# Rows of the first expert visit gathered on TensorE instead of through memory, in a two-layer graph and mixture-of-experts network

## What is computed

```python
scores = softmax(xt @ wg + bg)                       # 1024 x 8
routing_weights, selected = top_2_with_jitter(scores)
for e in range(8):
    h = gelu(xt @ w1[e]) * (xt @ w3[e])              # 512 -> 1024
    out = out + comb[:, e:e+1] * (h @ w2[e])         # 1024 -> 512
```

## Time and profile before

| | us |
|---|---|
| median of 3 runs | 1915.27 |
| lowest and highest | 1909.77, 1923.55 |
| the profiled execution | 1906.49 |
| its span in the profile | 1904.7 |

### The profile page before, as it was taken

One profiled execution on the slowest core, in us unless ns is written; L12 is line 12 of the kernel. 1 busy time (PEld: TensorE's weight loads), 2 busy tenths in 40 slices (PEclk: granted clock), 3 DMA queues, 4 the chain that ended last, 5 costly groups with the idle time before them and its releaser, 6 DMA issues.

```text
span 1904.7 us, 19746 instructions
## 1 busy us (share of the span) xinstructions
PE 1707.0 (90%) x7679; PEld 1322.5 (69%) x7679; DVE 1101.8 (58%) x1835; ACT 673.7 (35%) x879; POOL 1000.7 (53%) x546
## 2 busy tenths in 40 slices
PE   6998999999896699999998299999999859999996
PEld 5664567788764456788886178787777747887863
DVE  7597758999875476756327433423433266623275
ACT  3323534332421244243331255655555412221112
POOL 3224561466778667548860456667676480152402
PEclk9999989999999688899999599999999979999988
DMA  8362111455332211122351767787777341121001
GB/s 331 95 207 50 1 1 48 122 111 111 62 78 22 23 1 1 23 67 45 66 160 34 260 204 264 250 275 246 247 270 240 136 122 45 45 89 43 24 1 45
DMA packets 146780, 212.56 MB, mean 112 GB/s; under 512 B 43740, under 2 KB 60352, under 8 KB 145440
## 3 DMA queue, kind: packets, MB, share of 16 engines
q1 hardware_dynamic: 98736, 177.49, 28.6%
q0 software_dynamic: 42832, 18.84, 8.3%
q10 hardware_dynamic: 5120, 14.99, 2.3%
HBM read 187.21 MB, written 30.08 MB: 114 GB/s over the span
## 4 chain that ended last, share of the span: by engine, by line
PE 65%; DVE 14%; POOL 6%; DMA 5%; ACT 5%; issue 4%; SPq 0%; POOLq 0%; DVEq 0%
PE PS L634 17%; PE PS L636 17%; PE PS L635 17%; PE PS L799 5%; PE PS L813 3%; DMA table_c<-edge_add,edge_ix 2%; POOL table_w L2293 2%; POOL table_c L2293 2%; PE PS L790 2%; ACT kd L1308 2%; PE PS L782 2%; DMA table_w<-edge_add,edge_ix 1%; POOL W L2218 1%; DVE h_op L1946 1%; POOL slots_x L2327 1%
## 5 line engine op out<-in xcount | busy, mean ns | idle before, releaser
L2218 POOL TENSOR_TENSOR W<-raw,W 128x2048 fp32r<-128x2048 f32 x40 | 192.4, 4813 | 330.8 <-ACT W L1158 323.6
L2293 POOL DMA_INDIRECT table_w<-edge_add,edge_ix x128 | 208.6, 1630 | 69.8 <-DMA table_w<-edge_add,edge_ix 39.7
L2293 POOL DMA_INDIRECT table_c<-edge_add,edge_ix x128 | 204.6, 1598 | 60.8 <-issue 33.5
L634 PE MATMUL PS<-op_b,W 128*128 128x512 f32 x576 | 225.5, 392 | 3.6 <-DVE op_b L2025 2.6
L635 PE MATMUL PS<-op_b,W 128*128 128x512 f32 x576 | 224.4, 390 | 0.0
L636 PE MATMUL PS<-op_b,W 128*128 128x512 f32 x576 | 224.4, 390 | 0.0
L634 PE MATMUL PS<-W,op_a 128*128 128x512 f32 x480 | 188.2, 392 | 2.9 <-DVE op_a L1755 1.8
L635 PE MATMUL PS<-W,op_a 128*128 128x512 f32 x480 | 187.1, 390 | 0.0
L636 PE MATMUL PS<-W,op_a 128*128 128x512 f32 x480 | 187.0, 390 | 0.0
L2332 POOL TENSOR_TENSOR W<-raw,W 128x2048 fp32r<-128x2048 f32 x30 | 143.5, 4792 | 56.4 <-ACT W L1389 56.4
L1158 ACT ACTIVATE W<-raw 128x2048 fp32r<-128x2048 f32 x40 | 76.5, 1920 | 158.6 <-PE PS L636 103.3
(11 more groups left out here) (419 smaller groups left out, 3824.2 us busy)
## 6 DMA issues: line engine op xcount, KB each, us to landing
raw<-in_L_ffn_w_dram SPq DMA_DIRECT2D x46, 1024.0 KB, 5.7
raw_e<-in_L_ffn_w_dram SPq DMA_DIRECT2D x22, 1024.0 KB, 5.9
raw_v<-in_L_ffn_w_dram SPq DMA_DIRECT2D x22, 1024.0 KB, 5.2
raw<-in_L_mix_W_dram SPq DMA_DIRECT2D x16, 1024.0 KB, 6.7
raw<-table_c SPq DMA_DIRECT2D x10, 1024.0 KB, 5.2
key_row<-key_dram SPq DMA_DIRECT2D x32, 256.0 KB, 4.0
w_row<-in_edge_weight_dram SPq DMA_DIRECT2D x32, 256.0 KB, 4.8
table_w<-zero POOLq DMA_DIRECT2D x4, 1024.0 KB, 7.9
```

The lines of the kernel that those rows point to most:

```text
L634: pe.matmul(ps, lhs_hi, rhs_hi, start=start, stop=False)
L2218: pool.tensor_tensor(lo_at, raw[:, r % 2, :], hi_at.bitcast(F32), ALU.subtract).then_inc(lo_done, 1)
L2293: pool.indirect_dma_start(out=tb, out_offset=bass.IndirectOffsetOnAxis(ap=edge_ix[:, i, c:c + 1].bitcast(U32), axis=0), in_=edge_add[:, i, ...
```

## The change

Four things change.

1. `expert_of` is computed before `slot_ix`: the seven instructions L1879 to L1887 are written after L1902.
2. The rows of visit 0 no longer come through memory. POOL writes the numbers 0 to 255 into `iota_v`. DVE takes for each token the smaller of its two slots (`slot_min`) and compares: `pick[:, t, s]` is 1 where token t*128+p has slot s, else 0, in eight instructions. PE multiplies the tiles of G, taken as the stationary operand, with `pick` in plain float32: 4 column blocks of G x 8 token tiles = 32 matmuls of 128x256. They give the transposed rows of visit 0 in two banks, and ACT and DVE split them into `x_op` as before.
3. SP no longer loads `x_slot` for visit 0. Its wait for `scattered_x` and the load for visit 1 stand ahead of block 5 instead of block 4. ACT and DVE split the rows of visit 0 after blocks 0 and 1 instead of after 0, 1 and 2. ACT's wait for `scattered_x` ahead of block 3 stays.
4. The eight matmuls with `ones` in job `rank` use float32r operands: `chosen` has that type, and ACT copies `ones` to `ones_r` once.

```diff
@@ SP
-                if b == RING:
+                if b == RING + 1:
                     sp.wait_ge(scattered_x, 16 * 2 * NT)
-                    load_x_slots(0)
                     load_x_slots(1)
@@ PE
+            pe.wait_ge(ones_ready, 1)
             for t in range(NT):
-                mm = pe.matmul(bank(n)[:, (t + 1) * EXPERTS:(NT + 1) * EXPERTS].rearrange("p (t e) -> p t e", e=EXPERTS), ones[:, :],
+                mm = pe.matmul(bank(n)[:, (t + 1) * EXPERTS:(NT + 1) * EXPERTS].rearrange("p (t e) -> p t e", e=EXPERTS), ones_r[:, :],
                                chosen[:, t, :].unsqueeze(1).to_broadcast([P, NT - t, EXPERTS]), start=False, stop=(t == NT - 1))
...
-            x_transposes(0)
-            evacuated("xT0", visit_tiles(0))
+            for j in range(2):
+                n = JOB["xT0"] + j
+                open_job(n)
+                for k in (2 * j, 2 * j + 1):
+                    for t in range(NT):
+                        if k == 0:
+                            pe.wait_ge(pick_ready, t + 1)
+                        mm = pe.matmul(bank(n)[:, (k % 2) * 2 * P:(k % 2 + 1) * 2 * P], G[:, t, k * P:(k + 1) * P], pick[:, t, :],
+                                       start=(t == 0), stop=(t == NT - 1))
+                mm.then_inc(job_full, 1)
+            evacuated("xT0", 2)
@@ ACT
-            for b in range(RING - 1):
+            for b in range(2):
                 block_to_hi(b)
-            x_hi(0)
-            block_to_hi(RING - 1)
+            for j in range(2):
+                n = JOB["xT0"] + j
+                act.wait_ge(job_full, n + 1)
+                act.activation(x_op[:, 0, :, 0, 2 * j * P:2 * (j + 1) * P].rearrange("p i (k s) -> p k i s", k=2),
+                               bank(n).rearrange("p (k i s) -> p k i s", k=2, i=2), ACT.Copy).then_inc(job_act, 1)
+            for b in range(2, RING):
+                block_to_hi(b)
@@ DVE
+            dve.wait_ge(iota_ready, 1)
+            link(dve.tensor_tensor(slot_min[:, :], slot_f[:, 0, :], slot_f[:, 1, :], ALU.min))
+            for t in range(NT):
+                dve.tensor_scalar(pick[:, t, :], iota_v[:, :], slot_min[:, t:t + 1], None, ALU.is_equal).then_inc(pick_ready, 1)
```

50 lines of the change are left out of this document (33 added, 17 removed).

## The result

| | before | after |
|---|---|---|
| median of 12 runs, us | 1916.29 | 1903.68 |
| lowest and highest | 1904.39, 1928.45 | 1894.94, 1911.79 |
| span of the profiled execution | 1904.7 | 1899.7 |
| ratio after / before | | 0.9928, 95% interval 0.9902 to 0.9954 |

The kernel became faster by 13.8 us by the ratio (12.6 by the medians). The forecast was 1898.3 us in 1889 to 1908, with a gain of 17.0 us. The time is in the range, and it is within 1% of before, the likeliest of the three cases; about 3 us of the forecast's gain are missing. The times alone don't show that they are: the interval of the ratio is a gain of 8.8 to 18.8 us, which has the 17.0 in it. What is missing is read from the traces.

A forecast was written before the change was run, and what follows sets the result against it. PE was taken to set the pace, standing 36.3 us until visit 0's rows were loaded. 15.3 + 2.5 - 0.8 = 17.0 us off the median 1915.27 gave 1898.3 us, range 1889 to 1908 (1893 to 1903 from the gain alone).

The forecast's parts named there:

- What bounds the kernel: Expert stage: once visits run, PE sets their pace, so a later start of visit 0 ends the kernel equally later.
- Rival D: Later visits, bound by weights, give back visit 0's earlier start, so no effect; chance 0.02.
- Rank: Job rank on PE: float32r leaves one record for each product, 8 fewer at 0.21 us, 1.7 us less.
- Experts before slots: DVE in routing: `expert_of` ready 3.4 us earlier, `slot_ix` 1.5 us later.
- Picks and gather: Ahead of visit 0: first pick about 0.5 us after `slot_ix`, then every 0.29; PE's 64 gather records take 16.1 us.
- Rival B: PE's clock stays at 1.2 GHz in the gather, which takes 27.5 us; gain 4 to 6.3 us; chance 0.07.
- g0 of visit 0: Its first product on PE starts at 1074.4 instead of 1089.75, 15.3 us earlier.
- Up to g0 of visit 1: Visit 0's 15.3 us plus 2.5 us of its first products at full clock: 17.8 us, less 0 to 0.4.
- S: Time at which the scatter has landed, 1082.56 before; forecast from 1084.1 to 1086.7.
- Rival A: The scatter lands only at 1088 to 1094 and holds visit 0; gain 9 to 15 us; chance 0.13.
- What is late next: Visit 1's rows and blocks 3 to 5 wait for the scatter; 0.5 us off, with 0.3 for small things.
- Rival C: Slower: the later scatter, sharing engines with a fifth block, lands after 1101.6 and delays g0 of visit 1; chance 0.02.

The follow-up runs named there:

- e3: The changed kernel with the eight products of job rank in plain float32 again; ratio to before 0.9950.
- e4: The kernel before with only `expert_of` computed ahead of `slot_ix`; ratio to before 1.0019.
- e2: The changed kernel with the slots computed ahead of the experts again; ratio to before 0.9918.
- e1: The changed kernel with DVE's gating of visit 0's second half of hidden rows ahead of the low part of block 6; ratio to before 0.9921.
- c1: The changed kernel once more, unedited, for the spread; ratio to before 0.9929.
- f6: The changed kernel with ACT's gelu of g0 of visit 0 ahead of the high part of block 3; ratio to before 0.9880.
- f3: The changed kernel with DVE waiting for the scatter's end before the low part of block 2; ratio to before 0.9851.
- h4: h2 plus f3's wait of DVE for the scatter before the low part of block 2; ratio to before 0.9910.
- h2: The changed kernel with the orders of e1 and f6, and ACT making visit 1's rows ahead of block 6; ratio to before 0.9877.
- f4: The changed kernel with SP's wait for the scatter back ahead of block 4; ratio to before 0.9939.
- f1: e1 plus six thrown-away products on PE between job rank and the gather; ratio to before 0.9913.
- h1: h2 plus the six thrown-away products of f1; ratio to before 0.9912.

## Why the prediction was right, and where it was off

- **What bounds the kernel: right.** The visits kept their pace. The later waits are the same in both traces (1.01 and 0.69 us in turn), and what was gained at 80.8 is there at the end of the visits, 14.6 and 14.7 us. Rival D is out.
- **Rank, 1.7 us: right at the gather.** 1.85 us for 8 records; e3 gives the 1.7 back there. Further on it isn't shown.
- **Experts before slots: right in its times.** `expert_of` starts at 8.4 from chosen instead of 11.9, 3.4 us earlier, as forecast; `slot_ix` at 10.1 instead of 9.0, 1.1 us later (forecast 1.5). That the step is a loss by itself, and no gain with the rest of the change as it stands, the forecast didn't say; e4 and e2 show it.
- **Picks and gather: right.** The first pick 0.28 us after `slot_ix`, then 0.27 us each; 64 records in 16.23 us (forecast 16.1), the clock up after 4.4 us (forecast 4). Rival B is out.
- **g0 of visit 0: right.** 15.4 us earlier (forecast 15.3), and its products 0.23 us apart from the first on. Before, g0 to the first 0.69 us wait took 2.5 us over the clean 49.0; that is the forecast's 2.5 us of clock.
- **Up to g0 of visit 1: right.** 17.4 us earlier, against 17.8 less up to 0.4.
- **S: right.** Forecast were 1084.1 to 1086.7, which is 38.3 to 40.9 from chosen; it was 39.3 and 39.6. That is in part luck, as S was 36.4 in e1 with the same code ahead of it. The rule of the Trainium skill on the picks ("SBUF — State Buffer", "Who interferes with whom") would have made it up to 2.3 us later. The two scatters beside the picks took 1.12 and 1.08 us instead of 1.02 and 0.97 of the earlier trace rows, and the gap between them grew by nothing, so it was 0.2 us in all. Rival A, which rested partly on it, didn't occur: S would have had to be at 42.2 or later.
- **The term that was too small: "What is late next", which takes 0.8 us off the gain.** It asked only who needs S for visit 1's rows and for blocks 4 and 5, and there the margins held (PE waited 0.37 us). It didn't follow POOL's two low parts to the end and ask who runs beside them. DVE's block 6 does, is held until 1108.9, and behind it in DVE's order stand the hidden rows. What stood there before was a wait of 1.01 us; now it is 3.73, so the loss is 2.7 us. With the 0.37 it makes 3.1, nearly the 3.3 over clean of the table. In some executions (c1, e3) the clock falls behind it, in c1 with 2.4 us more lost. The term measured 3.1 to 5.7 us instead of 0.8. 17.8 less these gives 12 to 15 us, and 13.8 was measured.
- **The number: right by the width of the range.** 1903.7 us is just above the 1893 to 1903 that the forecast gives for its own mechanism, and its gain just under the 14 to 20. It lies in the 1900 to 1906 of rival A, whose mechanism the trace rules out. What covers it is the spread of a median that was added.
- **A reading that was wrong.** Rival C has g0 of visit 1 before at about 1112.6. In the trace it starts at 1114.64, so C's threshold for S is 2 us higher; it changes nothing else.

The hint was in the rows. The forecast read the earlier trace rows as "scatters stand still while DVE makes a low part" and used it for S alone, not for two low parts that meet. And they meet in the trace of the kernel before as well, where PE doesn't wait for it (POOL, then DVE):

```profile
1121.39 4.61 POOL L2332 TENSOR_TENSOR W<-raw,W 128x2048 fp32r<-128x2048 f32 x1
...
1124.00 4.15 DVE L1928 TENSOR_TENSOR W<-raw,W 128x2048 fp32r<-128x2048 f32 x1 [0.43 <-ACT W L1389]
```

POOL's ends at 1126.00, and DVE's takes 4.15 us instead of 2.29 and ends 2.15 us after that. A sentence on the same page and in the same section of the Trainium skill, "Who interferes with whom" in "SBUF — State Buffer", says it for this case: a DVE instruction with two SBUF inputs contends with a GpSimd instruction that reads SBUF. The rows agree, 5.63 us against 2.29, with DVE's instruction ending 2.15 us after POOL's.

**Shown and not shown.** That the 3.73 us come from DVE's order and the late S is shown by e1, f6, f3 and h4, each of which takes away a part of it or all. In h2 DVE's order is no longer what PE waits for, and the late S costs 3.08 us by way of block 8 on ACT instead. That the low parts of DVE stretch the scatters is shown by the count in f3 and h4. Open is when the clock falls: it did at or behind waits of 3.83 (c1), 3.29 (e3), 2.89 (f4) and 2.43 us (f1), and not at 3.73 (after) and 3.08 (h2). Open too are the late fall in five of the traces, what loading block 4 beside the scatter costs, and why the landing takes 2.8 to 3.0 us in four of the traces and 1.8 in nine.

## What to carry to other kernels

When a stall goes away, follow not only what is needed next but also which instructions of two engines run beside each other at a new place, and what stands in order behind each. Work out how long the group that was released late occupies its engine, lay the other engines' rows over that stretch, and charge the overlap to whoever waits behind. A gain at the start of a steady stage can be measured far better in the trace, from a mark inside the kernel, than in total times, if work ahead of the mark shifts by more than the change is worth. But run the unedited kernel twice: here its two executions differed by 4.2 us over that interval, more than most of the edits were worth.

## What the runs showed of the hardware

- Elementwise instructions of DVE and POOL on SBUF tiles of 128x2048 with two inputs took turns as whole instructions: DVE's 2.29 us became 5.63 and 5.74, POOL's 4.6 became 6.64, and DVE's ended 2.15 us after the end of POOL's (after, and before at 1124.00).
- The issue of an indirect transfer by POOL grew from 0.96 us to 1.9 to 3.1 us beside such an instruction of DVE, always to its end and 0.83 to 0.85 us more, and only to 1.12 and 1.08 us beside eight picks of 128x256.
- The last scatter landed 1.8 us after its issue had ended in nine traces (before, e1, e3, e4, f1, f3, f4, h1, h4), 2.8 to 3.0 us in four (after, c1, f6, h2), and 5.2 us in e2, where the issues ended earlier and the engines moved 410 GB/s or more until about 35 us from chosen.
- Matmul records of 8 to 64 columns took 0.21 us each at the lower clock (0.50, the 1.2 GHz level), float32r and float32 alike (8 in 1.85 us, 16 in 3.51).
